# 71 routed tiles for each half of the tokens, and sorted rows zeroed from 71 partitions

## Chip, cores and metric

One core of a Trainium2 chip runs the whole program. The metric is the device time of one execution in microseconds (us), lower is better; the median of several runs is given, and one more execution was profiled.

## What is computed

One transformer layer on 16 sequences of 512 tokens with 128 features: attention with 16 heads of 8 features, an ALiBi bias and a causal mask, then a residual and a layer norm; then a mixture of eight experts with a shared expert, again with residual and layer norm.

```python
x = _layernorm(x + attention(x))           # 16 heads, causal, bias by slope and distance
probs = softmax(xf @ gate_w.T)             # 8192 tokens, 8 experts
topw, topi = top_k(probs, 2); topw /= topw.sum(-1)
routed = sum over e of ffn_e(xf) * comb[:, e]     # each token in its two experts only
x = _layernorm(x + shared(xf) + routed)    # ffn: silu(x @ gate.T) * (x @ up.T) @ down.T, width 352
```

## The kernel before

The kernel has two blocks. The first is attention, the second the experts.

**Attention.** Every engine runs the same list of stages, `steps(...)`, with st.number from -3 to 16; stage st works on several sequences at once: it loads x three sequences ahead, makes the query and key stacks two ahead, takes the row maxima of the scores one ahead (and ten of forty two ahead), does scores, exponentials, masks and the product with v for sequence st, and normalises sequence st - 1. Within a stage the order is that of `plan(g)`, g from 0 to 3, on all engines. Of the stage's 40 score units on TensorE (lines 613 to 629), unit 0 waits for `max_rows` (line 617), that is, for the three transfers of lines 502 to 510 (`qstack<-mparts`), which put the negated row maxima into the query stack of the next sequence.

SyncE (SP) issues the transfers in this order in each stage (`body`, lines 476 to 513): the next x (`xin`) and the residual (`xres`), the stack loads (`load_stack`, line 489, thirteen transfers that wait for the split q and k), one transfer of zeros into a slice of `x_sorted` (lines 490 to 498), the three `mparts` transfers, and the store of the transposed result of the sequence before (`x1T`). In the last two stages there are no stack loads. After the stages SP loads the shared expert's weights and waits for them, for all zeroing transfers and for the stores (lines 516 to 520).

**Routing.** Tokens are handled in two halves (chunks) of 32 tiles of 128 tokens. DVE counts the tokens of each expert, rounds each group up to whole tiles of 128 and gives each of the 2 x 4096 token choices a row of `x_sorted[chunk]`; GpSimd (POOL) scatters the token rows there, those of the first half in stages 10 to 15 (from line 755 it waits for the first eight zeroing transfers), those of the second half in the expert block. A row has 128 features and a token id, 129 float32 or 516 bytes. Rows that no token is scattered to stay zero; their id gives a row number outside `y_tokens`, and their result is dropped.

**Experts.** One list of steps (`KINDS`): 24 shared steps, then CSLOT routed tiles for each half, then 24 shared steps. SP loads a tile five steps ahead, TensorE transposes it two steps ahead, its two products with the expert's weights, the transpose of the hidden values and the product with the down weights follow; POOL scatters the result to `y_tokens`. The first load of the second half waits for all of its scattered rows (line 1297). Mixing, the second layer norm and the stores of the output are tied to steps counted from CSLOT and NSLOT (`MIX`, line 962), and POOL's scatters to a plan counted the same way (`writes_by_step`).

At most 64 whole tiles and 7 partial ones are needed for a half, whatever the routing: 2 * CT + NE - 1 = 71. Before, this was rounded up to a multiple of TURN = 4, to 72.

Of the kernel before, what the change touches and what calls it, by code (L numbers as in the profile page):

```python
# [15 lines left out]
P = 128  # L16
B, T, C = 16, 512, 128
# [212 lines left out]
NE = 8  # L230
# [3 lines left out]
TURN = 4  # L234
CHUNKS = 2
CT = NTILE // CHUNKS
GROUPS = CHUNKS * NE


CSLOT = -(-(2 * CT + NE - 1) // TURN) * TURN  # L240
NSLOT = CHUNKS * CSLOT
RW = C + 1

# [109 lines left out]
def attention(nc, io, dram, keep):  # L353

    with ExitStack() as ctx:
# [6 lines left out]
        def sem(name):  # L362
# [6 lines left out]
        zeros = sb("zeros", [P, RW])  # L369
# [40 lines left out]

        names = """const_loaded masks_loaded late_loaded stack_rows_loaded0 stack_rows_loaded1 stack_rows_loaded2 const_ready unit_ready max_ready pv_ready xT_ps q_ps k_ps v_ps m_ps y_ps ynT_ps o_ps
            x1T_ps lg_ps exp_done xT_ready qk_high y_kept m_high ynT_ready x1T_ready max_taken rowmax_ready
            qk_split m_rest v_ready y_normed z_ready ln_done rstd_ready logits_kept zeros_set vaug_zeroed rows_zeroed masked qk_low res_biased x1_kept x_loaded0 x_loaded1 stats_passed maxima_passed exp_passed
            xres_loaded max_rows routed chosen prefix_ps placed places x_scattered ids_set routing_set x1T_stored shared_loaded""".split()
        S = {n: sem(n) for n in names}
        x_loaded = [S["x_loaded0"], S["x_loaded1"]]
# [15 lines left out]
        with nc.Block() as block:  # L432

            @block.sync
            def _(sp):
                def load(done, out, in_):
                    sp.dma_start(out, in_).then_inc(S[done], 16)

                load("const_loaded", ident[:], io["ident"])
                load("const_loaded", wq[:], io["q_w"])  # L440
                load("const_loaded", wkv_in[:], io["kv_w"])
                load("const_loaded", qb[:], io["q_b"].unsqueeze(1))
                load("const_loaded", kb[:], io["kv_b"][0:C].unsqueeze(1))

                def load_later():

                    for n in range(1, STACKS):
                        for stack, rows in ((qstack[n], io["qstack_rows"]), (kstack[n], io["kstack_rows"])):
                            for e in range(ORDERS - PROD):
                                if e or stack is kstack[n]:  # L450
                                    load(f"stack_rows_loaded{n}", stack[PROD + e:P:ORDERS, :, :].bitcast(U16), rows[e])
                    load("late_loaded", wo[:], io["o_w"])
                    load("late_loaded", ob[:], io["o_b"].unsqueeze(0).to_broadcast([P, C]))
                    with nc.allow_non_contiguous_dma(reason="the router's weights transposed"):
                        load("late_loaded", gw[:], io["gate_w"].rearrange("e c -> c e"))
                    load("late_loaded", keep["rank"][:], io["rank"].unsqueeze(0).to_broadcast([P, NE]))
                    load("late_loaded", keep["before"][:].bitcast(U16), io["before"])
                    load("late_loaded", keep["ids"][:], io["ids"])

                def load_stack(st):  # L460

                    buffer, done = st.stack(2), stack_loaded[st.stack(2)]
                    if st.number + 2 >= STACKS:
                        sp.wait_ge(S["unit_ready"], st.at(2 - STACKS, SEQ_UNITS, SEQ_UNITS))
                    sp.dma_start(qstack[buffer][PROD:P:ORDERS, :, :].bitcast(U16), io["qstack_rows"][0]).then_inc(done, 16)
                    for w, part in ((0, 0), (0, 1), (0, 2), (1, 0), (1, 1), (1, 2)):
                        stack, order = ((qstack[buffer], Q_PARTS), (kstack[buffer], K_PARTS))[w]
                        if part < 2:
                            sp.wait_ge(S["qk_high"], st.at(2, 4, 2 * w + part + 1))
                        else:  # L470
                            sp.wait_ge(S["qk_low"], st.at(2, 2, w + 1))
                        for n in range(len(order)):
                            if order[n] == part:
                                sp.dma_start(stack[n:P:ORDERS, :, :], parts[:, w, part, :]).then_inc(done, 16)

                def body(st):
                    if st.has(3):
                        if not st.first(3) and (st.every or st.number + 3 >= 2):

                            sp.wait_ge(S["xT_ps"], st.at(1, 1, 1))  # L480
                        sp.dma_start(xin[st.par(3)][:], io["x"][bass.ds(st.number + 3, 1)]
                                     .rearrange("b (i p) c -> p (b i) c", p=P)).then_inc(x_loaded[st.par(3)], 16)
                    if st.chained():
                        if not st.first(-1):
                            sp.wait_ge(S["z_ready"], st.at(-2, 1, 1))
                        sp.dma_start(xres[:], io["x"][bass.ds(st.number - 1, 1)]
                                     .rearrange("b (i p) c -> p (b i) c", p=P)).then_inc(S["xres_loaded"], 16)
                    if st.has(2):
                        load_stack(st)
                    if st.has(0):  # L490

                        if st.first(0):
                            sp.wait_ge(S["zeros_set"], 1)
                        chunk, turn = divmod(st.number * CHUNKS, B)
                        rows = CSLOT * P * CHUNKS // B
                        sp.dma_start(dram["x_sorted"][chunk][turn // CHUNKS * rows:(turn // CHUNKS + 1) * rows, :]
                                     .rearrange("(n p) c -> p n c", p=P),
                                     zeros[:].unsqueeze(1).to_broadcast([P, rows // P, RW])).then_inc(S["rows_zeroed"], 16)
                    if st.first(2):
                        load_later()  # L500
                    if st.has(1):
                        for a in range(PARTS):
                            row = ORDERS * (MAX_AT_ROW + a) + PROD
                            if a < 2:
                                sp.wait_ge(S["m_high"], st.at(1, 2, a + 1))
                            else:
                                sp.wait_ge(S["m_rest"], st.at(1, 2, 2))
                            sp.dma_start(qstack[st.stack(1)][row:row + ROWS + 1:ROWS, :, :]
                                         .rearrange("a u (i t) -> a (u i) t", t=P), mparts[:, a, :]) \
                                .then_inc(S["max_rows"], 16)  # L510
                    if st.chained():
                        sp.wait_ge(S["x1T_ready"], st.at(-1, 1, 1))
                        sp.dma_start(dram["x1T"][st.number - 1], x1T[:]).then_inc(S["x1T_stored"], 16)

                steps(sp, body)
                load("shared_loaded", keep["shared_in"][:], io["w_in"][:, NE, :, :])
                load("shared_loaded", keep["shared_down"][:], io["w_down"][:, NE, :, :])
                sp.wait_ge(S["shared_loaded"], 32)
                sp.wait_ge(S["rows_zeroed"], 16 * B)
                sp.wait_ge(S["x1T_stored"], 16 * (B - 1))  # L520

            @block.tensor
# [216 lines left out]
            def _(pool):  # L739
# [7 lines left out]
                def scatter_some(st, n):  # L747

                    choice = 0 if st.number < SCATTER_AT[1] else 1
                    if not SCATTER_AT[0] <= st.number < SCATTER_AT[0] + 6:  # L750
                        return
                    if n == 0 and st.number == SCATTER_AT[choice]:
                        pool.wait_ge(S["places"], 1)
                        if choice == 0:
                            pool.wait_ge(S["rows_zeroed"], 16 * B // CHUNKS)
                            pool.wait_ge(S["x1_kept"], CT // QT)
                        else:
                            pool.wait_ge(S["x_scattered"], 16 * CT)
                        pool.tensor_copy(keep["x1"][:, 0:CT, C:RW], keep["ids"][:, choice, 0:CT].unsqueeze(2)) \
                            .then_inc(S["ids_set"], 1)  # L760
                        pool.wait_ge(S["ids_set"], choice + 1)
                    if (n + 1) * 11 // SEQ_UNITS > n * 11 // SEQ_UNITS and scattered[choice] < CT:
                        scatter(pool, keep, dram, 0, scattered[choice], choice, S["x_scattered"])
                        scattered[choice] += 1
# [928 lines left out]
```

## Time and profile before

| | before |
|---|---|
| median of three runs | 1125.37 us (1124.48 to 1125.42) |
| profiled execution | 1125.76 us, of it 1124.0 us from the first to the last instruction |
| granted TensorE clock, mean | 0.966 |
| busy: TensorE, VectorE, ScalarE, GpSimd | 90%, 70%, 65%, 61% |
| attention block, about | 0 to 652 us |
| shared steps and setup, about | 652 to 730 us |
| routed tiles, about | 730 to 1035 us |
| shared steps, mixing, stores | to 1124 us |

PE is TensorE, DVE VectorE, ACT ScalarE, POOL GpSimd, SPq the queue on SyncE that issues transfers. The DMA share is the mean busy share of the core's 16 DMA engines; a single busy engine is 0.06. PEclk is the granted TensorE clock as a share of full speed. A number in brackets behind a line of the timeline is the time for which the engine stood idle before it, and who ended that.

### The profile page before, as it was taken

Reading aid. Unit: us, or ns where it says so; the run is one execution under the profiler, and the core shown is the slowest. Engines: PE = TensorE matmul, PEld = TensorE weight load, DVE = VectorE, ACT = ScalarE, POOL = GpSimd, SP = SyncE. Lnnn points to the kernel's source line nnn. Section 1 sums busy time; section 2 is a strip of 40 time slices with the busy share of each in tenths; the row PEclk is TensorE's granted clock in tenths of the full one; section 3 lists DMA queues with packets and bytes.
Section 4 is the critical chain, followed back from the end, with each engine's and each line's share of the span. In section 5 each row is a group of like instructions: output and inputs, shape, how many; then the busy total and the mean of one; then the engine's idle time right before and its main releaser. Section 6 shows DMA issues by size and latency. Waiting matters only on the chain. (4 is left out here: it accounts for less than half of the span.)

```text
span 1124.0 us, 28097 instructions
## 1 busy us (share of the span) xinstructions
PE 1011.1 (90%) x9268; PEld 701.8 (62%) x9268; DVE 784.6 (70%) x1943; ACT 726.0 (65%) x1578; POOL 685.0 (61%) x1191
## 2 busy tenths in 40 slices
PE   4999999999999988999899969899999999999981
PEld 1445444544454543544454348689999999999870
DVE  4898889888888988988898227634333335676585
ACT  1177767776677666677766834357777777887442
POOL 1045545554555544778777844868788887888421
PEclk9799999999999998999999989989999999999996
DMA  5233313432242222334231243122222223444233
GB/s 149 67 95 104 100 50 79 112 89 60 79 113 69 80 79 66 100 102 135 67 87 51 67 172 111 40 60 79 74 78 76 79 65 105 125 139 134 84 115 91
DMA packets 123597, 101.99 MB, mean 91 GB/s; under 512 B 18832, under 2 KB 114198, under 8 KB 122802
## 3 DMA queue, kind: packets, MB, share of 16 engines
q1 hardware_dynamic: 113650, 78.32, 25.9%
q0 software_dynamic: 8704, 16.87, 4.5%
q10 hardware_dynamic: 1104, 5.01, 1.1%
q8 instruction: 80, 1.31, 0.5%
q14 instruction: 59, 0.48, 0.2%
HBM read 39.44 MB, written 35.79 MB: 67 GB/s over the span
## 5 line engine op out<-in xcount | busy, mean ns | idle before, releaser
L712 ACT ACTIVATE probs<-scores 128x512 f32<-128x512 f32 x640 | 344.6, 602 | 82.4 <-PE scores L626 80.4
L778 POOL TENSOR_SCALAR_AFFINE_SELECT probs<-probs 128x256 f32<-128x256 f32 (+1 forms) x640 | 224.8, 364 | 189.2 <-ACT probs L712 177.6
L921 DVE TENSOR_REDUCE rowmax<-maxed 128x1 f32<-128x512 f32 (+1 forms) x384 | 246.1, 683 | 36.0 <-PE maxed L609 34.3
L603 PE MATMUL maxed<-kstack,qstack 64*128 64x512 bf16 (+3 forms) x1024 | 218.1, 315 | 40.7 <-DVE maxB L921 20.3
L1219 DVE TENSOR_TENSOR e_hid<-e_gate,e_up_ps 128x352 f32<-128x352 f32 (+2 forms) x192 | 107.6, 560 | 185.4 <-ACT e_gate L1498 158.5
L626 PE MATMUL scores<-qstack,kstack 64*128 64x128 bf16 (+3 forms) x1024 | 221.3, 302 | 12.2 <-ACT probs L712 11.9
L642 PE MATMUL pv<-probs,vaug 128*32 128x512 f32 (+3 forms) x2048 | 192.8, 449 | 2.9 <-POOL probs L778 2.9
L921 DVE TENSOR_REDUCE maxB<-maxed 128x4 f32<-128x512 f32 x256 | 162.1, 680 | 19.9 <-PE maxed L609 19.5
L1593 POOL DMA_INDIRECT y_tokens<-e_raw,e_row_i x144 | 142.7, 991 | 38.5 <-issue 27.2
L609 PE MATMUL maxed<-causal,halves 64*128 64x128 bf16 (+1 forms) x1280 | 160.1, 212 | 0.0
L1498 ACT ACTIVATE e_gate<-e_gate_ps 128x352 f32<-128x352 f32 (+2 forms) x192 | 95.2, 496 | 83.9 <-PE e_gate_ps L1395 48.4
L609 PEld LDWEIGHTS maxed<-causal,halves 64*128 64x128 bf16 x1280 | 114.8, 98 | 50.8 <-issue 9.9
L626 PEld LDWEIGHTS scores<-qstack,kstack 64*128 64x128 bf16 x1024 | 72.2, 94 | 101.1 <-ACT probs L712 71.1
L1460 PE MATMUL e_y_ps<-e_w_down,e_hT 128*128 (+1 forms) x864 | 120.7, 276 | 0.0
L1405 PE MATMUL e_gate_ps<-e_w_in,e_xT 128*128 x432 | 106.7, 355 | 5.0 <-POOL e_w_in L1540 5.0
L1460 PEld LDWEIGHTS e_y_ps<-e_w_down,e_hT 128*128 128x128 f32 (+1 forms) x864 | 108.4, 192 | 0.1
L603 PEld LDWEIGHTS maxed<-kstack,qstack 64*128 64x128 bf16 x1024 | 60.6, 95 | 61.5 <-DVE maxB L921 27.2
L1405 PE MATMUL e_up_ps<-e_w_in,e_xT 128*128 x432 | 94.4, 327 | 0.0
L1510 ACT ACTIVATE e_hT<-e_h_ps 128x384 f32<-128x384 f32 x144 | 70.6, 490 | 8.0 <-PE e_h_ps L1448 1.1
L1405 PEld LDWEIGHTS e_up_ps<-e_w_in,e_xT 128*128 128x128 f32 x432 | 74.9, 191 | 0.0
L1448 PE MATMUL e_h_ps<-ident,e_hid 128*128 128x128 f32 x432 | 70.9, 273 | 1.7 <-DVE e_hid L1219 1.7
L348 POOL DMA_INDIRECT x_sorted<-x_all,place_best x64 | 63.0, 985 | 15.2 <-issue 13.2
(183 smaller groups left out, 1595.0 us busy)
## 6 DMA issues: line engine op xcount, KB each, us to landing
qstack<-parts SPq DMA_DIRECT2D x96, 128.0 KB, 2.5
kstack<-parts SPq DMA_DIRECT2D x96, 128.0 KB, 2.5
x_sorted<-zeros SPq DMA_DIRECT2D x16, 580.5 KB
e_xs<-x_sorted SPq DMA_DIRECT2D x144, 64.5 KB
e_raw<-y_tokens SPq DMA_DIRECT2D x64, 128.0 KB
xin<-in_x SPq DMA_DIRECT2D x16, 256.0 KB, 3.0
e_group_in<-x1T_all SPq DMA_DIRECT2D x16, 256.0 KB, 2.7
out<-e_raw SPq DMA_DIRECT2D x64, 64.0 KB
```

The costliest lines, as they stand in the source:

```text
L603: pe.matmul(bank[:, col:col + (i + 1) * P], q[rows, slot, i * P:(i + 1) * P], ks[rows, slot, 0:(i + 1) * P], start=first, stop=False, skip ...
L609: done = pe.matmul(diagonal[:, :, half, :], halves[rows, half, :], causal[rows, 0:1 if kind == 0 else 2, :], start=False, stop=half == 1, ...
L626: last = pe.matmul(scores[st.at(0, SEQ_UNITS, n) % SB][:, col:col + width], ks[rows, slot, kt * P:(kt + 1) * P], q[rows, slot, kt * P:T], ...
L642: last = pe.matmul(pv[hh * VW:(hh + 1) * VW, kt * P:T], vaug[st.par(off)][:, kt, g * QUAD + hh, :], probs[g % 2][:, at * T + col:at * T + ...
L712: act.activation(probs[g % 2][:, u * T:(u + 1) * T], scores[st.at(0, SEQ_UNITS, UNITS * g + u) % SB][:], ACT.Exp).then_inc(S["exp_done"], 1)
L778: pool.affine_select(out=view, in_=view, compare_op=ALU.is_ge, fill=0.0, base=0, pattern=pattern, channel_multiplier=-1).then_inc(S["maske ...
L921: dve.tensor_reduce(out, keys, AX.X, ALU.max).then_inc(S["max_taken"], 1)
L1219: dve.tensor_tensor(hid[step % len(hid)][rows, 0:cols], gate[step % 2][rows, 0:cols], up_ps[step % 2][rows, 0:cols], ALU.mult).then_inc(S[ ...
L1405: done = pe.matmul(bank[:, 0:F], xT[n % len(xT)][:, x_part, :], w_in[:, e, w, w_part, :].rearrange("p a f -> p (a f)"), start=m == 0, stop ...
L1460: done = pe.matmul(y_ps[:, 0:C], hT[n % 2][0:fw, j * P:(j + 1) * P], w_down[0:fw, e, j, :].rearrange("p a c -> p (a c)"), start=j == 0, st ...
L1498: act.activation(gate[step % 2][rows, 0:cols], gate_ps[step % 2][rows, 0:cols], ACT.Silu).then_inc(S["silu_done"], 1)
L1593: pool.indirect_dma_start(out=dram["y_tokens"][n // CSLOT], out_offset=bass.IndirectOffsetOnAxis(ap=row_i[:, n:n + 1], axis=0), in_=ys[:, ...
```

## The change

CSLOT becomes 71. Two routed tiles fall out of the list of steps, one for each half, and all that is counted from the number of tiles moves with it. The slice of `x_sorted` that one transfer zeroes is 1136 rows in place of 1152; before it was written from 128 partitions, nine rows each, and now from 71 partitions, sixteen rows each (row n * 71 + p from partition p). The semaphore `rows_zeroed` is split in two, one for each half.

```diff
-CSLOT = -(-(2 * CT + NE - 1) // TURN) * TURN
+CSLOT = 2 * CT + NE - 1
 NSLOT = CHUNKS * CSLOT
...
                         rows = CSLOT * P * CHUNKS // B
                         sp.dma_start(dram["x_sorted"][chunk][turn // CHUNKS * rows:(turn // CHUNKS + 1) * rows, :]
-                                     .rearrange("(n p) c -> p n c", p=P),
-                                     zeros[:].unsqueeze(1).to_broadcast([P, rows // P, RW])).then_inc(S["rows_zeroed"], 16)
+                                     .rearrange("(n p) c -> p n c", p=CSLOT),
+                                     zeros[0:CSLOT].unsqueeze(1).to_broadcast([CSLOT, rows // CSLOT, RW])) \
+                            .then_inc(S[f"rows_zeroed{chunk}"], 16)
...
-                sp.wait_ge(S["rows_zeroed"], 16 * B)
+                sp.wait_ge(S["rows_zeroed1"], 16 * B // CHUNKS)
...
-                            pool.wait_ge(S["rows_zeroed"], 16 * B // CHUNKS)
+                            pool.wait_ge(S["rows_zeroed0"], 16 * B // CHUNKS)
```

## Rows read from the trace of the kernel before

**Rows 1.** Windows: busy us (x instructions) per engine, PEclk, DMA share, GB/s.

```profile
160.00:200.00 40.00, 37.23 (x431) 19.82 (x430) 34.95 (x73) 29.60 (x58) 21.18 (x50) 1.00 0.32 88
...
800.00:840.00 40.00, 40.00 (x310) 39.59 (x309) 14.88 (x57) 29.11 (x77) 33.60 (x41) 1.00 0.28 77
```

**Rows 2.** Timeline of TensorE: start, us, line; unit 0 of four stages.

```profile
162.92 0.39 PE L626 MATMUL scores<-qstack,kstack 64*128 64x512 bf16 x1
...
200.49 0.39 PE L626 MATMUL scores<-qstack,kstack 64*128 64x512 bf16 x1
...
589.57 0.39 PE L626 MATMUL scores<-qstack,kstack 64*128 64x512 bf16 x1
...
622.74 0.53 PE L626 MATMUL scores<-qstack,kstack 64*128 64x512 bf16 x2
```

**Rows 3.** Timeline of the SP queue: start, us of issuing, line, transfer.

```profile
176.06 0.60 SPq L496 DMA_DIRECT2D x_sorted<-zeros  x1
194.98 2.38 SPq L508 DMA_DIRECT2D qstack<-mparts  x3
```

**Rows 4.** The page: one DMA queue; issues with count, KB each, us to landing.

```profile
q1 hardware_dynamic: 113650, 78.32, 25.9%
...
x_sorted<-zeros SPq DMA_DIRECT2D x16, 580.5 KB
...
qstack<-mparts SPq DMA_DIRECT2D x48, 16.0 KB
...
shared_down<-in_w_down SPq DMA_DIRECT2D x1, 192.0 KB, 3.7
```

**Rows 5.** Windows (columns of rows 1) in a zeroing transfer and in an mparts transfer.

```profile
177.50:178.00 0.50, 0.50 (x11) 0.37 (x4) 0.50 (x2) 0.50 (x2) 0.22 (x1) 1.00 1.09 314
...
178.50:179.00 0.50, 0.50 (x15) 0.36 (x15) 0.47 (x3) 0.36 (x1) 0.18 (x1) 1.00 1.09 282
...
198.05:198.50 0.45, 0.45 (x12) 0.25 (x9) 0.37 (x1) 0.45 (x2) 0.45 (x1) 1.00 0.15 35
```

**Rows 6.** Timeline of the SP queue, other zeroing transfers and the last load.

```profile
71.56 0.59 SPq L496 DMA_DIRECT2D x_sorted<-zeros  x1
...
101.76 0.59 SPq L496 DMA_DIRECT2D x_sorted<-zeros  x1
...
566.56 0.59 SPq L496 DMA_DIRECT2D x_sorted<-zeros  x1
...
589.06 0.51 SPq L496 DMA_DIRECT2D x_sorted<-zeros  x1
...
622.08 0.36 SPq L496 DMA_DIRECT2D x_sorted<-zeros  x1
...
650.55 0.44 SPq L437 DMA_DIRECT2D shared_down<-in_w_down  x1
```

**Rows 7.** Windows around clock drops, and the TensorE wait that ended at 731.32.

```profile
303.90:310.70 6.80, 6.21 (x41) 1.92 (x36) 5.55 (x13) 3.67 (x9) 2.59 (x8) 0.50 0.00 1
...
655.70:661.50 5.80, 0.06 (x5) 0.02 (x1) 0.54 (x3) 1.30 (x3) 0.14 (x2) 0.78 0.00 0
...
661.50:665.70 4.20, 3.75 (x16) 2.98 (x16) 2.59 (x9) 0.81 (x2) 1.21 (x1) 0.50 0.65 190
...
731.32 1.25 PE L1405 MATMUL e_gate_ps<-e_w_in,e_xT 128*128 x3 [4.97 <-POOL e_w_in L1540]
...
730.60:737.40 6.80, 6.08 (x24) 5.95 (x25) 1.00 (x4) 1.23 (x4) 5.84 (x8) 0.50 0.19 51
```

**Rows 8.** The chain that ended last: start, us, who; two routed tiles.

```profile
973.51 0.67 PE e_y_ps L1460 x6
975.60 0.67 PE e_y_ps L1460 x6
```

**Rows 9.** Waits of the SP queue (us, times, longest), and its timeline there.

```profile
SPq L1302 <- DMA x_sorted<-x_all,place_second: 3.0, 1, 3.0
...
879.27 1.51 SPq L1302 DMA_DIRECT2D e_xs<-x_sorted  x3
```

More of the change, by code:

```diff
@@ L412, in attention @@
             x1T_ps lg_ps exp_done xT_ready qk_high y_kept m_high ynT_ready x1T_ready max_taken rowmax_ready
-            qk_split m_rest v_ready y_normed z_ready ln_done rstd_ready logits_kept zeros_set vaug_zeroed rows_zeroed masked qk_low res_biased x1_kept x_loaded0 x_loaded1 stats_passed maxima_passed exp_passed
+            qk_split m_rest v_ready y_normed z_ready ln_done rstd_ready logits_kept zeros_set vaug_zeroed rows_zeroed0 rows_zeroed1 masked qk_low res_biased x1_kept x_loaded0 x_loaded1 stats_passed maxima_passed exp_passed
             xres_loaded max_rows routed chosen prefix_ps placed places x_scattered ids_set routing_set x1T_stored shared_loaded""".split()
```

## Prediction, made before the changed kernel was run

> **What bounds the kernel now.** I read the 40 us windows first. In a window of the attention part TensorE is busy 37.23 of 40 us, in one of the routed part 40.00 of 40 [rows 1], so both are bound by TensorE's own order of work, and whatever makes it wait is added to the time in full. The attention part is a loop over 16 sequences, one stage each. A stage starts with unit 0 of its scores on TensorE: 162.92 and 200.49, 37.6 us apart [rows 2]. Unit 0 may not start before all 48 x stage counts of `max_rows` are in (line 617), that is, before the three small transfers `qstack<-mparts` have landed. So I read the SP queue next, because those three are issued by SP behind the zeroing transfer of the same stage: `x_sorted<-zeros` at 176.06, `qstack<-mparts` at 194.98 to 197.4 [rows 3], the next unit 0 at 200.49. That margin of some 2 us is what the change has to be held against.
>
> **How a transfer is spread over the DMA engines.** The zeroing moves 580.5 KB in 16 transfers [rows 4]. While one runs, the 16 engines are all busy (share 1.09) and move 314 GB/s [rows 5]. The transfer `qstack<-mparts` is another matter: 64 partitions of 256 B into a destination whose outermost dimension is 2. While it runs the share is 0.15 at 35 GB/s [rows 5]; two engines of 16 are 0.125, or 0.16 with the overlap that also makes the full share read 1.09 and more. So the outermost sizes decide: 128 and 128 use all engines, 64 and 2 use two. The new zeroing transfer has 71 outermost on both sides, and 71 is prime: no split into 2, 4, 8 or 16 equal shares exists. I take it that all 71 x 16 = 1136 row pieces go to one engine, the first of those that also carry `mparts`.
> The Trainium skill, "DMA: Bandwidth & Descriptors", section "Why a DMA increments its semaphore by 16 and not by 1", has the rule in words: the number of engines is the largest up to 16 that divides the slowest dimension of both sides, always counted from the lowest engine. By that rule 64 and 2 give two, in agreement with the row, and 71 gives one. The same section speaks of copies issued by GpSimd that are spread in unequal shares; this one is issued by SP, and no run here shows the difference.
>
> **The price of one zeroing transfer.** At 314 GB/s each of 16 engines moves 19.6 GB/s, so a piece of 516 B takes 26.3 ns; at the 282 GB/s of the next row 29.3 ns [rows 5]. The SP queue's whole traffic, 78.32 MB in 25.9% of 16 x 1124 us, gives 30.7 ns for 516 B [rows 4]. I take 28 ns, between the two rows of the transfer itself, and 26.3 and 30.7 as ends: 1136 x 28 = 31.8 us (29.9 to 34.9), in place of 72 x 28 = 2.0 us on each engine.
>
> **What waits behind it.** I take it that the engine works through SP's queue in order (rival C is the other case). SP issues the zeroing 13.1 us after unit 0 (176.06 - 162.92) [rows 2, 3]; a late one, at 566.56, stands 23.0 before the next unit 0 at 589.57, so 14.6 after its own [rows 2, 6]. I use 13.7. The new period of a stage, from unit 0 to unit 0, is then: 13.7 to the issue, 1.2 from issue to the first piece (an estimate: the third `mparts` issue begins near 196.9, the last 0.5 of the 2.38 us from 194.98, and its bytes move in the window from 198.05 [rows 3, 5]), 31.8 for the zeroing, 1.4 for the three `mparts` trains (32 pieces each at 14 ns: 16 KB on two engines at 35 GB/s is 0.47 us [rows 4, 5]), 0.3 for the semaphore. That is 48.4 us, of which the last 34.7 follow the issue. Everything else that SP puts behind it (x1T store, next x, residual, constant rows) lands right after and is needed later in the next stage; the stack loads of a stage stand before its zeroing.
> The sum over the stages, by issue times of the zeroing [rows 6], and the unit 0 after them [rows 2]:
> first to second, 71.56 to 101.76: 48.4 - 30.2 = +18.2;
> second to fourteenth, 101.76 to 566.56, twelve periods: 12 x 48.4 - 464.8 = +116.0 (the one long stage with the routing is inside: there the wait is nearly hidden);
> fourteenth to the next unit 0, 566.56 to 589.57: 34.7 - 23.0 = +11.7;
> fifteenth, issued at 589.06, just before its unit 0, so that it ends 34.2 us after it, where the stage takes 33.2: +1.0;
> last, issued at 622.08: done 32.3 us after unit 0 at 622.74, and the two shared-weight loads that SP waits for at the block's end (issued at 650.55, landed 3.7 later [rows 4, 6]) now land behind it, at 35.8 in place of 31.5: +4.3.
> Together +151.2 us.
>
> **The clock.** Each of 14 stages now begins after about 10 us in which TensorE stands still. What that does to the granted clock is shown by two waits of before. After the stretch 655.7 to 661.5, nearly idle, the level is 0.50 (1.2 GHz) for another 4.2 us of work; after the wait of 4.97 us that ends at 731.32 it is 0.50 until 737.4, 6.1 us [rows 7]. Otherwise the attention part runs at 1.00 (2.4 GHz) [rows 1]. At half clock in the attention part 41 matmuls run in 6.8 us, at full clock 431 in 40 us, or 73 in 6.8: 3.0 us of 6.8 are lost, 0.43 of each [rows 1, 7]. 4.2 to 6.1 us at that rate are 1.8 to 2.6; I take 2.2, x 14 = +30.8. Ends: nothing, where VectorE and ScalarE, which catch up in the wait, give back what the clock takes; 5.9 (13.7 x 0.43), where the half level lasts through the 13.7 us up to the issue, which is the part that counts for the chain.
>
> **The two tiles fewer.** A routed tile is 2.08 us of TensorE (975.60 - 973.51 is 2.09, and 310 matmuls in 40 us at 16 to a tile are 2.06 [rows 1, 8]), nothing waits in it, and all later steps, mixing and stores included, are numbered from the tile count: -4.2. Against it: the first load of the second half waits for the last scattered row (3.0 us of SP's waiting, then the issue at 879.27 [rows 9]), and its transpose is now one step earlier, 2.08 us before the present one and some 2.2 after that issue; against about 2 us to land it is late by 0 to 0.5: +0.3. The two result scatters and the two columns less in the expert table lie beside TensorE: nothing. The semaphores: POOL's first wait is met two stages ahead, SP's last was counted above: nothing.
> Sum: 151.2 + 30.8 - 4.2 + 0.3 = +178.1, on 1125.8 for the profiled execution, 1303.9; that execution lies 0.4 above the median, so 1303.5.
>
> **The rivals.**
> A, the forecast, 0.83. With the ends: 29.9 in place of 31.8 takes 1.9 x 16 = 30 off, a clock term of nothing another 31, so 1243; 34.9 adds 50, a clock term of 5.9 adds 52, so 1406.
> B, the other side, 0.10: the 1136 pieces are spread over all engines anyway (by the 16 rows of each partition, or 5 partitions to an engine), 71 to 80 pieces each. The price is then that of before, 2 us 19 us ahead of `mparts`, and only the tiles are left: 1125.8 - 3.9 = 1121.9, by the median 1121.5, faster by 0.35%. For it: nothing more than that 1136 is a multiple of 16. Against it: the two-engine row, where 64 pieces were not spread over 16 either. It decides at the first zeroing transfer: 2.5 us or 30.
> C, 0.06: one engine, but `mparts` does not stand behind it (another engine, or a queue that takes turns). Then only the load of that engine counts: 0.32 of 37.6 us in use before [rows 1] is 12.0, less 2.0, plus 31.8, is 41.8 us a stage against 37.6, 15 x 4.2 = +63, 1185. Against it: both are on SP's queue, and the two engines of `mparts` are two of 16.
> The Trainium skill, same page, section "Queues, rings and completion order", says that each engine takes the pieces of one queue in ring order, which speaks for A over C; no row of before has a long transfer ahead of a short one.
> The remaining 0.01 is for anything near no change.
>
> **How the numbers follow.** Predicted 1303.5, that of A. Range 1235 to 1400: A with its bounds; B and C stay outside, as does the corner where both unknowns stand at their upper end, so about 2 in 10 are left out. About 0.2% is what a measurement of this kernel tells from no change. Faster 0.10 (B), within 0.2% 0.01, slower 0.89 (A and C).
>
> **What would show it.** In the profile after: stages 48 to 51 us apart in place of 37.6; TensorE waiting 9 to 12 us at line 626, or at the score unit of line 617, for a DMA, once a stage, after which the clock is at half for some us; a DMA share of about 0.06 at 18 to 20 GB/s for some 32 us after each zeroing issue in place of 1.09 for 2.3 us; routed tiles still 2.08 us apart and two fewer. Wrong would be: stages still at 37.6 (B), stages near 42 with the wait at another transfer (C), or a piece that takes over 31 ns when one engine works alone.

## The result, and the profile after

The changed kernel takes 1365.68 us (median of 6 runs, 1362.87 to 1366.7), the kernel before 1125.39 in the same comparison: a ratio of 1.2131, 95% interval 1.2105 to 1.2158. The profiled execution is 1364.4 us from the first to the last instruction, 240.4 longer than before. The forecast was 1303.5 with a range of 1235 to 1400; direction and mechanism are as forecast, the size was 62 us too small.

The page of the changed kernel (TensorE's busy time is 1040.2 us where it was 1011.1, although two tiles have gone, and its share of the span falls from 90% to 76%; in part 5, the score matmuls now wait for a DMA):

```profile
PE 1040.2 (76%) x9236; PEld 705.1 (52%) x9236; DVE 782.1 (57%) x1937; ACT 726.1 (53%) x1570; POOL 683.0 (50%) x1188
...
PEclk9688797897986978879879688869999999999996
...
L627 PE MATMUL scores<-qstack,kstack 64*128 64x128 bf16 (+3 forms) x1024 | 233.7, 315 | 222.2 <-DMA qstack<-mparts 210.0
```

TensorE's longest wait in the changed kernel (us in total, times, longest); it has no counterpart before:

```profile
PE scores L627 <- DMA qstack<-mparts: 210.0, 15, 22.9
```

Fifteen waits, one for each stage from the second on. Two neighbouring ones, in TensorE's timeline; they are the ones that stood at 162.92 and 200.49 [rows 2], and are 53.3 us apart in place of 37.6:

```profile
164.44 0.60 PE L627 MATMUL scores<-qstack,kstack 64*128 64x512 bf16 x1 [14.90 <-DMA qstack<-mparts]
...
217.70 0.60 PE L627 MATMUL scores<-qstack,kstack 64*128 64x512 bf16 x1 [13.98 <-DMA qstack<-mparts]
```

SP's queue in that stage, against [rows 3]. The second number is how long SP was in the instruction; the row of `mparts` is the first of the three alone:

```profile
179.25 0.45 SPq L496 DMA_DIRECT2D x_sorted<-zeros  x1
198.15 13.54 SPq L509 DMA_DIRECT2D qstack<-mparts  x1
```

Windows inside the same stage (busy us of the engines, PEclk, DMA share, GB/s), against [rows 5]:

```profile
185.00:195.00 10.00, 8.90 (x103) 4.69 (x101) 8.29 (x22) 6.09 (x12) 4.26 (x12) 1.00 0.08 18
...
205.60:217.60 12.00, 0.00 (x0) 0.00 (x0) 0.00 (x0) 0.00 (x0) 0.00 (x0) 0.50 0.26 73
217.60:222.60 5.00, 4.90 (x28) 1.82 (x28) 1.45 (x3) 1.95 (x4) 0.59 (x2) 0.50 0.17 51
222.60:260.20 37.60, 32.23 (x369) 16.98 (x366) 31.23 (x66) 25.47 (x50) 18.86 (x44) 1.00 0.21 55
```

Where the zeroing of before used all 16 engines at 282 to 314 GB/s and was through in 2.7 us, one engine now moves 17 of the 18 GB/s. In the trace's records of single pieces its 1136 pieces start from 180.57 to 215.03, over 34.46 us or 30.4 ns apart. The same records show who stands behind them. `mparts` has 192 pieces, 96 on each of two engines: 96 run from 212.34 to 213.80, beside the zeroing, and the other 96 only when its last piece is done at 215.06. It is 96 and 96 in every one of the fifteen stages. TensorE does nothing in 205.6 to 217.6 and works the first 5 us after it at the 1.2 GHz level.

The 240.4 us, split at three marks of the trace: from the first stage's unit 0 to the last one's +239.9 (58.90 to 862.68, before 58.86 to 622.74); from there to the first routed tile's transpose +5.7 (105.7 against 100.1); through the routed tiles, first to last transpose, -5.2 (303.2 against 308.3); after them -0.1. Nearly all of the loss is in the attention part, and the two tiles fewer do bring something.

### The profile page after: what moved, and what is told of

Read it like the earlier page. It is cut to its first block and busy times, and to the rows that moved or that the text cites. A ratio compares the mean times of both kernels' runs of the same rounds, so it can differ in the third digit from the quotient of the medians.

```text
span 1364.4 us, 27978 instructions
## 1 busy us (share of the span) xinstructions
PE 1040.2 (76%) x9236; PEld 705.1 (52%) x9236; DVE 782.1 (57%) x1937; ACT 726.1 (53%) x1570; POOL 683.0 (50%) x1188
## 5 line engine op out<-in xcount | busy, mean ns | idle before, releaser
L627 PE MATMUL scores<-qstack,kstack 64*128 64x128 bf16 (+3 forms) x1024 | 233.7, 315 | 222.2 <-DMA qstack<-mparts 210.0
L604 PE MATMUL maxed<-kstack,qstack 64*128 64x512 bf16 (+3 forms) x1024 | 228.5, 327 | 40.1 <-DVE maxB L922 20.3
L643 PE MATMUL pv<-probs,vaug 128*32 128x512 f32 (+3 forms) x2048 | 208.9, 483 | 2.9 <-POOL probs L779 2.9
L610 PE MATMUL maxed<-causal,halves 64*128 64x128 bf16 (+1 forms) x1280 | 165.0, 217 | 0.0
L610 PEld LDWEIGHTS maxed<-causal,halves 64*128 64x128 bf16 x1280 | 118.0, 102 | 57.6 <-issue 21.4
L604 PEld LDWEIGHTS maxed<-kstack,qstack 64*128 64x128 bf16 x1024 | 61.1, 96 | 60.4 <-DVE maxB L922 27.1
```

Source lines behind the costliest of these rows:

```text
L604: pe.matmul(bank[:, col:col + (i + 1) * P], q[rows, slot, i * P:(i + 1) * P], ks[rows, slot, 0:(i + 1) * P], start=first, stop=False, skip ...
L610: done = pe.matmul(diagonal[:, :, half, :], halves[rows, half, :], causal[rows, 0:1 if kind == 0 else 2, :], start=False, stop=half == 1, ...
L627: last = pe.matmul(scores[st.at(0, SEQ_UNITS, n) % SB][:, col:col + width], ks[rows, slot, kt * P:(kt + 1) * P], q[rows, slot, kt * P:T], ...
L643: last = pe.matmul(pv[hh * VW:(hh + 1) * VW, kt * P:T], vaug[st.par(off)][:, kt, g * QUAD + hh, :], probs[g % 2][:, at * T + col:at * T + ...
```

## Experiments

My theory, T: 71 is prime, so the transfer runs on one DMA engine; `mparts` is behind it in SP's queue; unit 0 waits for `mparts`. Rivals: few source partitions, or the order of the rows, are slow by themselves; the tile count costs something; only the engine's load in sum counts, not the order. The ranges of stage lengths below leave out the first and the last stage, which are shorter, and the one with the routing where it is longer.

**The shape undone.**

```diff
-                                     .rearrange("(n p) c -> p n c", p=CSLOT),
-                                     zeros[0:CSLOT].unsqueeze(1).to_broadcast([CSLOT, rows // CSLOT, RW])) \
+                                     .rearrange("(n p) c -> p n c", p=16),
+                                     zeros[0:16].unsqueeze(1).to_broadcast([16, rows // 16, RW])) \
```

> The changed kernel with one thing undone: the 1136 rows of a zeroing transfer are written from 16 partitions with 71 rows each, not from 71 with 16. Same rows, same bytes, same 516 B pieces, 71 routed tiles. My theory (a prime outermost size puts the whole transfer on one DMA engine, and the mparts transfers stand behind it): all 16 engines work, the burst takes 2.3 to 2.7 us in place of 34.4, stages are 37.6 us apart, and only the two tiles are left: 1121.5 us, 0.3 to 0.4% under the kernel before. Rival (fewer source partitions, or rows written in another order, are slow by themselves, since every row now comes from 16 instead of 71 partitions): as slow as the changed kernel or slower, 1365 or more.

Measured: 1120.65 us, ratio to before 0.9961 (0.9943 to 0.998). Two unit 0 in TensorE's timeline:

```profile
163.20 0.39 PE L627 MATMUL scores<-qstack,kstack 64*128 64x512 bf16 x1
...
200.78 0.39 PE L627 MATMUL scores<-qstack,kstack 64*128 64x512 bf16 x1
```

and a window in the zeroing between them:

```profile
178.00:184.00 6.00, 6.00 (x66) 3.61 (x67) 5.88 (x13) 4.14 (x8) 2.89 (x8) 1.00 0.80 86
```

Stages are back at 37.6 us, and what is left is the gain of the two tiles. This kernel is faster than both, and 0.39% faster than the kernel before. One thing was not as expected: the engines are busy (share 0.80), but at 86 GB/s, and the burst takes 7.0 us and not 2.5. That costs nothing here, it is over 10.7 us before `mparts` is issued in the stage shown, but it wanted a reason; the experiments with partitions apart are for it.

**The shape alone, with 72 tiles.**

```diff
-CSLOT = 2 * CT + NE - 1
+CSLOT = 72
+LONE = 71
...
+                        for first, count, width in ((0, 16, 16), (16, 16 * LONE, LONE)):
+                            sp.dma_start(dram["x_sorted"][chunk][at + first:at + first + count, :]
+                                         .rearrange("(n p) c -> p n c", p=width),
+                                         zeros[0:width].unsqueeze(1).to_broadcast([width, count // width, RW])) \
```

> 72 routed tiles for each half as before, but the zeroing of a stage in two transfers: 16 rows from 16 partitions, then 1136 rows from 71 partitions. The shape of the transfer alone, without the tile count. My theory: all of the loss is in the shape, so the time is that of the changed kernel plus two routed tiles, 1365.7 + 4.2 = 1370 us (1364 to 1376), stages 53 to 56 us apart. Rival (the count of 71 and what is numbered from it costs something of its own): clearly under 1365.

Measured: 1367.21 us in one run (1370 expected, 1364 to 1376), stages 53.6 to 56.7 us. The shape alone, with 72 tiles, gives the whole loss, and the first experiment gives the whole gain without it: the shape costs 245 us (1365.7 - 1120.7), the tiles bring 4 (1124.5 - 1120.7). The 1.5 us between this run and the changed kernel are less than the 3.8 over which the latter's runs spread, and say nothing of the tiles.

**Fewer pieces on the one engine.**

```diff
+                        for first, count, width in ((0, 4 * CSLOT, 4), (4 * CSLOT, 12 * CSLOT, CSLOT)):
+                            sp.dma_start(dram["x_sorted"][chunk][at + first:at + first + count, :]
+                                         .rearrange("(n p) c -> p n c", p=width),
+                                         zeros[0:width].unsqueeze(1).to_broadcast([width, count // width, RW])) \
```

> The changed kernel with the zeroing of a stage split: 4 of 16 rows of each set from 4 partitions (71 pieces on each of 4 engines), then the other 12 from 71 partitions (852 pieces on one engine), so 923 of the 1136 pieces are on the loaded engine. My theory (a chain: issue 13.2 us after unit 0, 1.2, 923 x 30.4 ns = 28.1, 2.7 until unit 0 can start, that is 45.2 us against 37.6, and 2 to 4 us for the clock) gives 9 to 12 us less per stage than the changed kernel's 54.7 only by the pieces, 6.5 each: stages of 46 to 48 us, 1365.7 - 15 x 6.5 = 1268 us (1240 to 1275). Rival (only the load of that engine counts: 10 us of other work + 28.1 = 38 us a stage): stages of 38, 1128.

Measured: 1324.55 us in one run, stages of 50.4 to 54.2: above the expected 1240 to 1275, below the changed kernel, and far from the rival's 1128. A row of TensorE's timeline:

```profile
212.08 0.60 PE L629 MATMUL scores<-qstack,kstack 64*128 64x512 bf16 x1 [11.79 <-DMA qstack<-mparts]
```

and a window in the small transfer from 4 partitions:

```profile
178.00:183.00 5.00, 5.00 (x61) 2.98 (x60) 4.88 (x12) 3.62 (x7) 2.23 (x6) 1.00 0.22 24
```

The chain held and the time of the pieces did not. In the stage from 160.99 to 212.08 the zeroing runs from 177.12 to 209.62: 16.1 to the first piece, 32.5 for the pieces where 28.1 were expected, 2.5 to unit 0, together 51.1. The 284 pieces from 4 partitions keep four engines busy (share 0.22), but the four together move 24 GB/s, 21 of them for these pieces, so that 147 KB take some 6.7 us where 71 pieces an engine at 30.4 ns would be 2.2. The same surprise as in the first experiment.

**Another queue.**

```diff
-                        sp.dma_start(dram["x_sorted"][chunk][turn // CHUNKS * rows:(turn // CHUNKS + 1) * rows, :]
...
+                        if g == 0 and st.has(0):
...
+                            act.dma_start(dram["x_sorted"][chunk][turn // CHUNKS * rows:(turn // CHUNKS + 1) * rows, :]
```

> The changed kernel with the zeroing transfer of 71 partitions issued by ScalarE, at the end of the first quarter of a stage, so that it is in another queue of the same DMA engine than mparts. If the engine takes turns between queues, mparts waits little, and what is left is the load of the engine, 34.4 us + some 10 of other work = 44.5 us a stage: 1121 + 15 x 6.9 = 1225 us (1170 to 1260), with waits at the stack loads or at ScalarE's issue. If the engine finishes one transfer before it takes another, whatever the queue, stages stay at 50 to 55 us: 1300 to 1370.

Measured: 1208.57 us in one run, stages of 40.8 to 43.5 us. The waits of TensorE for `mparts` shrink from 210.0 us to this:

```profile
PE scores L617 <- DMA qstack<-mparts: 47.0, 15, 4.3
```

One whole stage as a window:

```profile
178.03:220.34 42.31, 36.44 (x393) 18.59 (x393) 32.69 (x68) 27.35 (x53) 19.40 (x46) 0.94 0.28 76
```

The same transfer, still on one engine, costs 88 us in place of 245 when it does not stand in front of `mparts`: the engine takes turns between the two queues. In the records of the pieces `mparts` is issued from 211.67 on and its last piece is done at 219.78, while pieces of the zeroing run on to 229.97, past unit 0 at 220.34. So about two thirds of the loss is the order. The rest is 71 us in the stages and some 14 after them, where SP waits 20.2 us for the last zeroing transfer (profile against profile of the first experiment). Stages of 42 to 43 are in line with the load of the one engine, which was estimated at 44.5; that it is the load was not tested by itself.

**Two engines, neighbouring partitions.**

```diff
-                                     zeros[0:CSLOT].unsqueeze(1).to_broadcast([CSLOT, rows // CSLOT, RW])) \
+                                     zeros[0:2].unsqueeze(1).to_broadcast([2, rows // 2, RW])) \
```

> The changed kernel, zeroing from partitions 0 and 1 with 568 rows each, so two DMA engines with 568 pieces each. It asks two things. First the chain: what ends before the mparts transfers are issued, some 19 us after the zeroing, costs nothing. Second, why 16 neighbouring partitions moved only 86 GB/s on 16 engines and 4 neighbouring ones some 25 GB/s on 4 engines, where one engine alone moves 17 to 18. If each engine keeps its own 30.4 ns a piece, the transfer takes 17.3 us and is hidden: 1121 us. If neighbouring partitions share a way out of 22 to 25 GB/s, it takes 586 KB / 23.5 = 25 us (23 to 27), a stage is 13.2 + 1.2 + 25 + 2.7 = 42 us and some 2 for the clock, against 37.6: 1121 + 15 x 6.4 = 1217 us (1180 to 1240).

Measured: 1246.45 us in one run, above the expected 1180 to 1240, stages of 43 to 50.1 us; the reading follows with the next one, which has to be held against it.

**Two engines, partitions 0 and 64.** The source is `zeros[0:P:64]`, all else as in the one above.

> The same two engines with 568 pieces each, but from partitions 0 and 64 in place of 0 and 1. If neighbouring partitions share a way out, these two do not: 568 x 30.4 ns = 17.3 us, over before mparts is issued, stages 37.6 us, 1121 us (1118 to 1128). If two engines are slow together for another reason (the rows they write, the engines themselves), the same as from partitions 0 and 1. If the loss of the changed kernel were one of the engine's load in sum and not of the order, nothing changes by these 17 us either, since 10 + 17.3 is under 37.6.

Measured: 1126.55 us in one run. Windows inside a transfer, first of partitions 0 and 1:

```profile
213.00:239.00 26.00, 20.66 (x241) 11.59 (x239) 20.85 (x48) 15.90 (x32) 11.23 (x29) 0.97 0.13 24
```

and of partitions 0 and 64:

```profile
187.00:203.00 16.00, 13.98 (x156) 7.48 (x153) 14.10 (x35) 10.00 (x19) 7.29 (x19) 1.00 0.16 37
```

Two engines are busy in both (0.13 and 0.16 of 16). From neighbouring partitions they move 24 GB/s, 22 of them for this transfer, which takes 23 to 31 us. From partitions apart they move 37 GB/s, 34 of them for this transfer, twice the one engine's 17, and it takes 17.1 to 17.8 us, up to 19.2 where GpSimd scatters. That is over when `mparts` is issued, and from the third stage on the stages are 37.6 to 37.9 us, but for the routing one. The 6 us over the first experiment are in the first two, 34.7 and 40.2 against 28.6 and 38.2: in the first, `mparts` follows the zeroing much sooner, and TensorE's list has one wait for it, of 6.1 us. (This is a single run, and those of the first experiment spread from 1116.5 to 1124.0.) The 1246 was over my 1217: 42 + 2 for a stage was worked out, and a usual one took 16.3 to the first piece, 27.1 for the pieces and 2.7, or 46.

**Sixteen partitions apart.** As the first experiment, with `zeros[0:P:8]` as the source.

> The changed kernel, zeroing from 16 partitions as in the first experiment, but every eighth one (0, 8, ... 120) in place of 0 to 15. If groups of neighbouring partitions share a way out, the burst moves 150 to 250 GB/s in place of 86 and takes 2.4 to 3.9 us in place of 6.7; otherwise 6.7 as before. The total in both cases 1120.5 us (1118 to 1123), since 6.7 us are hidden already: 0.3 to 0.4% under the kernel before.

Measured: 1120.65 us, ratio 0.997 (0.9949 to 0.9992), so no different from the first experiment's in time. A window in the burst:

```profile
176.50:179.00 2.50, 2.50 (x34) 1.52 (x34) 2.47 (x7) 1.85 (x4) 1.58 (x4) 1.00 0.95 178
```

178 GB/s in place of 86, 3.7 to 4.0 us in place of 7.0. The reason is therefore in the source. What the zeroing pieces alone move in these windows: 4 partitions in a row 21 GB/s, 2 in a row 22, 16 in a row 86, 2 apart 34, 16 apart 178. The Trainium skill, "SBUF — State Buffer", section "Door 1: The DMA port swizzle (why `[64,N]` ≈ `[32,N]`)", has a map for this: four neighbouring partitions lie on one of 16 ports, the partition 32 further on the same one, the one 64 further on another. By it partitions 0 to 15 reach 4 ports and 0, 8, ... 120 reach 8. The trace agrees in the ratio: 21.5 and 22.3 GB/s for each port, where the page gives 27 for large transfers.

**Another place in SP's order.**

```diff
-                    if st.has(2):
-                        load_stack(st)
                     if st.has(0):
...
+                    if st.has(2):
+                        load_stack(st)
                     if st.first(2):
```

> The changed kernel with the slow transfer at another place of SP's order: ahead of the stage's stack loads in place of behind them. The mparts transfers have nothing slow in front of them then, the stack loads have. In the changed kernel SP's next issue was held for 13.5 us until some 110 pieces were left, so the stack loads will be issued only from 32 us after the start of the stage and land near 41; the first maximum of the last quarter, 28.2 us into the stage, waits for them, and 9.4 us of the stage follow: stages of 50 to 54 us, 1310 to 1370 us, with the wait of TensorE at the maxima and for kstack. If SP were not held and only the engine's order counted, the loads land at 38: stages of 47 to 49, 1265 to 1300.

Measured: 1340.54 us in one run, stages of 51.6 to 54.6 us, within the expected 1310 to 1370. TensorE's longest wait in the list of waits:

```profile
PE maxed L604 <- DMA kstack<-parts: 205.5, 15, 19.3
```

SP's timeline at the start of a stage:

```profile
212.22 0.37 SPq L494 DMA_DIRECT2D x_sorted<-zeros  x1
212.64 32.69 SPq L465 DMA_DIRECT2D qstack<-in_qstack_rows  x1
```

The wait moves to whatever stands behind the slow transfer, here the key stack, at nearly the same price. It also shows that SP itself is held: its next issue lasts 32.7 us, until 245.33, while the pieces run until 248.65. In the changed kernel it was held until 211.69 with the pieces running until 215.03. Both times 3.3 us, or 110 pieces, were left; over all stages of both runs in which SP was held it is 109 to 118. In the changed kernel this hold adds nothing to the wait of unit 0: all three `mparts` are issued by 213.64, before the last zeroing piece at 215.03.

**Rows that follow one another.**

```diff
-                                     .rearrange("(n p) c -> p n c", p=CSLOT),
+                                     .rearrange("(p n) c -> p n c", p=CSLOT),
```

> The changed kernel, still from 71 partitions, but each partition writes 16 rows that follow one another in memory, not 16 rows that are 71 rows apart. The one engine took 30.4 ns a piece where 16 engines took 28 each. If the distance of the rows written makes the difference, the piece falls to 28 ns or less, the transfer to 31.8 us, a stage by 2.6 us: 1365.7 - 16 x 2.6 = 1324 us. If it is the engine or its source, which partition after partition has one way out, nothing changes: 30.4 ns, 34.4 us, 1362 to 1370 us.

Measured: 1368.39 us in one run, and the same rate in a window:

```profile
185.00:195.00 10.00, 8.90 (x101) 5.36 (x99) 8.26 (x22) 6.57 (x13) 3.27 (x10) 1.00 0.08 18
```

34.45 us and 30.4 ns a piece: the distance of the rows is not what makes a lone engine slower than each of sixteen. What does is open. The two engines of partitions 0 and 64 took the same, 30.3 ns a piece (568 in 17.23 us).

## Why the prediction was right, and where it was short

**What bounds the attention part, and the margin of `mparts`:** right. The wait is at unit 0, for `qstack<-mparts`, 15 times; the two changes of queue and of place show that the order makes it. It is 14.0 us on average (210.0 / 15) where 9 to 12 were forecast, and the stages are 53.3 to 56.4 us apart where 48 to 51 were, for the two reasons that follow.

**One engine for 71 partitions:** right. The DMA share is 0.08 (0.06 for the one, the rest overlap as in [rows 5]), and 16 partitions in place of 71 take the loss away. The two-engine row of `mparts` was enough to see it.

**The price of a piece:** too low, and the main error. I took 28 ns from the rates of sixteen engines together [rows 5]; a lone one takes 30.4, close to the 30.7 that I had as the upper end [rows 4] (by luck: that was an average over all transfers of the queue), and 31.8 to 32.8 in the stages in which GpSimd scatters, which my sum had not taken into account at all, and which is over the 31 ns named as a sign of being wrong. A transfer is 34.45 us ten times and 36.1 to 36.7 five times, against 31.8: 10 x 2.65 + 5 x 4.6 = 50 us of the missing 62. That the scatters slow it is read from the stages they run in and was not tested by itself.

**What follows the transfer:** 1.4 + 0.3 us were put down, and 2.3 to 3.1 measured, most often 2.6 (215.03 to 217.70 is 2.67): 15 x 0.95 = 14 us. By the records of the pieces, the 96 pieces of `mparts` behind the zeroing take 1.5 to 1.7 us, so the 1.4 was near. From the last of them to unit 0 it is another 0.8 to 1.3, most often 1.1, and this is where the 0.3 "for the semaphore" failed: no row stood behind it. What the 1.1 us consist of is open.

**The way to the issue, and the clock:** right. From unit 0 to the first piece 13.7 + 1.2 + 2.2 = 17.1 were forecast, and 16.1 to 18.1 measured, 17.1 on average over the thirteen stages from the second to the fourteenth; before, the same thirteen have 15.0, so the stall adds 2.1 us. The half level lasts 4.9 us after unit 0 in the stage shown (217.7 to 222.6), within the 4.2 to 6.1 of [rows 7], and 2.8 to 6.2 in the others. The first 5 us of a stage, before:

```profile
200.49:205.49 5.00, 5.00 (x48) 2.02 (x49) 2.88 (x6) 3.18 (x7) 1.90 (x6) 1.00 0.36 106
```

In the changed kernel 28 matmuls run in such 5 us, where 48 did: 2.1 us lost, 2.2 forecast. TensorE's busy time says the same: 29.0 us more than in the first experiment (1040.2 against 1011.2) for the same 9236 matmuls.

So the attention part was forecast at 151.2 - 4.3 + 30.8 = +177.7 and came to +239.9; 50 and 14 are the difference and 2 more.

**The end of the block:** +5.7 for +4.3, and that they are near is in part luck. The last transfer has 37.2 us and ends 37.9 after unit 0, not 32.3; the down weights of the shared expert land 40.4 after it (903.13), where 35.8 was forecast and 31.6 was the time before, so 8.9 later. Before, though, SP's next issue comes 6.5 us after that landing (660.79), and now 3.0 (906.09): some 3.5 of the delay fall into room that the forecast did not know of.

**The tiles:** -5.2 for -3.9, of two errors against each other. The first transpose of the second half was to be late by 0 to 0.5 us, for +0.3. SP waits longer for the last scattered row than the 3.0 of [rows 9], and TensorE now waits as well; from the two lists of waits:

```profile
SPq L1303 <- DMA x_sorted<-x_all,place_second: 6.5, 1, 6.5
PE e_x_ps L1424 <- DMA e_xs<-x_sorted: 1.3, 1, 1.3
```

The two transposes there are 3.54 us apart in place of 2.08, so +1.5. Against it some 2.9 us are won between the third transpose and the thirteenth, for which the forecast had nothing; there the granted clock is at the half level once, for 3.4 us (977.0 to 980.4), and before it was for 6.8 (730.6 to 737.4) and again for 3.4 (754.5 to 757.9). That the clock is all of it was not tested. With the shape mended the two tiles are worth 0.39% (0.2 to 0.57).

**The rivals:** B was what the mended kernel does, 1121.5 forecast and 1120.65 measured. C, that only the load counts, is false for the changed kernel, and comes near once the transfer is in ScalarE's queue: 1185 worked out there, with the 28 ns, and 1208.57 measured.

## What to carry to other kernels

Before a transfer's shape is changed, look at the outermost size on both sides: 128 or 16 kept all 16 DMA engines at work, while 71, a prime, left one, and a transfer of 2.7 us that nobody waited for became one of 34 us. Then ask what is issued behind it in the same queue and how many us later; here it was 19 us, so that a transfer of 17 cost next to nothing and one of 27 a stall in nearly every stage. Price a single engine by a row in which a single engine works, or keep the upper bound: the rate of one out of sixteen was 8% off, which with fifteen links in a chain is 40 of the 62 us. And leave no term of a repeated chain without a row, however small: 0.3 us in place of 1.1 was another 12.

## What the hardware showed that I had not expected

A lone DMA engine took 30.4 ns for a piece of 516 B (17.0 GB/s), whether its rows followed one another or not, where each of sixteen, reading 128 partitions, took 27 to 29 (298 and 273 pieces in the windows of 0.5 us in [rows 5]).

Neighbouring source partitions share a way out: two engines reading partitions 0 and 1 moved 22 GB/s together, reading 0 and 64 34 GB/s; sixteen reading 0 to 15 moved 86, reading every eighth 178.

SP can be held by a slow transfer: it stayed in its next DMA issue for 13.5 and 32.7 us, in both cases until about 110 pieces of the transfer before were left. SP issues in order, so what it would have issued next was held as well.
